# Router products with the padded router weights stationary on four column groups

## The reference

```python
x = layernorm(x + attention(x))          # 16 query heads, 4 key/value heads, head size 32, rotary on half
x = layernorm(x + mlstm(x, ctx, ctx))    # 16 heads, gates from [q, k, v], a running sum and maximum over time
x = layernorm(x + ffn(x))

# ffn: 16 experts, top 2, plus one shared expert
logits = flat @ router_w.T                               # 4096 x 512 by 512 x 16
scores = softmax(logits)
_, topk_idx = top_k(logits + router_bias, 2)
topk_scores = take_along_axis(scores, topk_idx); topk_scores /= topk_scores.sum(-1)
for e in range(16):
    out += combine[:, e] * ((silu(flat @ Wu[e]) * (flat @ Wg[e])) @ Wd[e])
out += (silu(flat @ Su) * (flat @ Sg)) @ Sd              # shared expert, inner size 512
```

## Time and profile before

| | us |
|---|---|
| median of 3 runs (2013.22 to 2020.41) | 2019.02 |
| the profiled execution, whole | 2020.32 |
| its span, first to last instruction | 2018.8 |
| TensorE busy | 1835.8 (91%) |
| VectorE busy | 1143.9 (57%) |
| ScalarE busy | 644.5 (32%) |
| GpSimd busy | 691.1 (34%) |
| mean granted TensorE clock | 0.961 of full |

### The profile page before, as it was taken

How to read it: one execution, slowest core, us unless ns; L and a number is a source line. 1 busy time by engine, 2 the same in 40 slices (tenths; PEclk the granted TensorE clock), 3 DMA queues, 4 the chain that set the end, 5 groups by cost and what they waited for, 6 DMA issues and landing times.

```text
span 2018.8 us, 35358 instructions
## 1 busy us (share of the span) xinstructions
PE 1835.8 (91%) x10992; PEld 1176.2 (58%) x10993; DVE 1143.9 (57%) x2407; ACT 644.5 (32%) x1355; POOL 691.1 (34%) x752
## 2 busy tenths in 40 slices
PE   3879999999999999999999999998789999999990
PEld 1556675766657576675766657576455444454440
DVE  1467766767677677767767676676432222222225
ACT  0142433335233352433435243342312212221224
POOL 4034232342423324232342423322224444444440
PEclk7789999999999999999999999998899999999995
DMA  8154342444424344242444424333415576656549
GB/s 283 43 119 113 59 122 73 93 113 92 122 63 102 89 100 121 62 122 73 92 114 92 122 56 109 82 85 73 147 43 129 111 187 171 126 120 145 93 74 342
DMA packets 151421, 225.94 MB, mean 112 GB/s; under 512 B 31889, under 2 KB 106641, under 8 KB 148817
## 3 DMA queue, kind: packets, MB, share of 16 engines
q1 hardware_dynamic: 102048, 132.94, 25.0%
q0 software_dynamic: 38112, 91.86, 19.9%
q10 hardware_dynamic: 11216, 0.61, 0.4%
HBM read 94.44 MB, written 48.57 MB: 71 GB/s over the span
## 4 chain that ended last, share of the span: by engine, by line
PE 77%; DVE 11%; issue 4%; ACT 3%; DMA 2%; SPq 1%; POOL 1%; DVEq 0%; ACTq 0%; POOLq 0%
PE ps L1606 14%; PE ps L1159 11%; PE ps L1097 8%; PE ps L1625 7%; PE ps L1386 6%; PE ps L1361 5%; PE ps L1245 4%; PE ps L1281 3%; PE ps L1350 3%; DVE arden L898 3%; PE ps L1228 3%; DVE smax L880 3%; PE ps L1111 2%; PE ps L1207 2%; PE ps L1594 2%
## 5 line engine op out<-in xcount | busy, mean ns | idle before, releaser
L1606 PE MATMUL ps<-ug_w,rowsT 128*128 x632 | 289.5, 601 | 8.0 <-SPq L1455 4.6
L489 POOL DMA_INDIRECT routed_ids<-pair_w,pos_w x64 | 64.1, 1001 | 453.8 <-DVE pair_w L776 409.4
L1606 PEld LDWEIGHTS ps<-ug_w,rowsT 128*128 128x128 f32 x632 | 121.5, 193 | 162.0 <-issue 162.0
L1495 POOL DMA_INDIRECT sum_rows<-y_sb,pairs x79 | 125.8, 1592 | 247.4 <-DVE y_sb L1573 125.1
L880 DVE TENSOR_REDUCE smax<-ps 128x2 f32<-128x512 f32 x256 | 163.5, 679 | 26.4 <-PE ps L1281 26.4
L1097 PE MATMUL ps<-wqkv_sb,xT_sb 128*128 128x256 f32 (+1 forms) x512 | 172.2, 489 | 6.0 <-DMA wqkv_sb<-in_wqkv 6.0
L898 DVE RECIPROCAL arden<-ps 128x256 f32<-128x256 f32 x64 | 112.5, 1758 | 114.2 <-PE ps L1350 104.6
L1561 DVE SCALAR_TENSOR_TENSOR silu<-tanh,ps 128x256 f32<-128x256 f32 x79 | 33.3, 421 | 249.8 <-ACT tanh L1516 249.8
L990 DVE SCALAR_TENSOR_TENSOR weighted<-ps,decay 128x384 f32<-128x384 f32 x256 | 140.1, 553 | 60.6 <-PE ps L1228 51.4
L633 ACT ACTIVATE decay<-ps,g_col 128x256 f32<-128x256 f32 x256 | 121.6, 475 | 137.8 <-PE ps L1209 100.6
L1281 PE MATMUL ps<-k_stack,q_stack 96*128 96x256 f32 x512 | 113.3, 326 | 41.8 <-DMA q_stack<-qkT_lo 25.8
(11 more groups left out here) (253 smaller groups left out, 3636.7 us busy)
## 6 DMA issues: line engine op xcount, KB each, us to landing
q_stack<-qkT_hi SPq DMA_DIRECT2D x128, 128.0 KB, 3.9
mk_stack<-ctxT_hi SPq DMA_DIRECT2D x128, 128.0 KB
mq_stack<-qkT_hi SPq DMA_DIRECT2D x128, 128.0 KB, 2.4
ug_w<-in_expert_ug SPq DMA_DIRECT2D x16, 1024.0 KB, 5.3
xT_sb<-in_xT SPq DMA_DIRECT2D x16, 512.0 KB, 3.2
x_sb<-in_x POOLq DMA_DIRECT2D x16, 512.0 KB, 3.8
ctxT_sb<-in_ctxT POOLq DMA_DIRECT2D x16, 512.0 KB, 3.9
ctx_sb<-in_ctx_in POOLq DMA_DIRECT2D x16, 512.0 KB, 7.7
```

Source lines behind the costliest of these rows:

```text
L1495: pool.indirect_dma_start(out=sum_dram, out_offset=bass.IndirectOffsetOnAxis(ap=tables.pairs[:, m, 0:1], axis=0), in_=y_sb[:, m % W, :], i ...
L1606: ins = nc.tensor.matmul(ps[:, 2 + k % 2, :], rowsT[:, k % 2, c, :], ug_w[:, bass.ds(slot, 1), c, :].rearrange("p o n -> p (o n)"), start= ...
```

## The change

The router weights become the stationary operand. `rw_sb` grows to 32 columns for each chunk, of which 16 are zeros. `route_chunks` makes four products of 256 tokens, one for each chunk of 128 rows, each on its own group of 32 columns of the array and so in its own 32 partitions of PSUM bank 4. These four partial products aren't accumulated. A new copy on ScalarE brings them into `lgT_sb`, which is the buffer `arden`. Then `route` makes two products, one for each token tile: `lgT_sb` is stationary, and `chunk_sum`, a matrix of zeros and ones made once at the start, sums the four chunks and turns the result to one row per token. `route_chunks` stands where `route` stood, and `route` now stands behind `gate_mm`.

```diff
-        rw_sb = sb("rw_sb", [P, KC, E])
+        rw_sb = sb("rw_sb", [P, KC, HD])
+        chunk_sum = sb("chunk_sum", [P, E])
...
+        lgT_sb = arden
...
-            late = [(wo_sb[:, :, :], wo), (rw_sb[:, :, :], router_w), (rb_sb[:, :], router_b.partition_broadcast(P)),
+            late = [(wo_sb[:, :, :], wo), (rw_sb[:, :, 0:E], router_w), (rb_sb[:, :], router_b.partition_broadcast(P)),
...
-            sp.wait_ge(consts.sem, 1)
+            sp.wait_ge(consts.sem, 2)
...
+            nc.gpsimd.memset(rw_sb[:, :, :], 0.0).then_inc(consts.sem, 1)
...
+                if w is not None:
+                    wait(act, lgT_ready, w, 1)
+                    nc.scalar.copy(lgT_sb[:, :], ps[:, 4, 0:S]).then_inc(lgT_done.sem, 1)
                 if y is not None:
                     wait(act, gabs_done, y, 1)
...
+            nc.vector.tensor_reduce(chunk_sum[:, :], id_sb[:, :].rearrange("p (j n) -> p n j", n=HD)[:, 0:E, :], AX.X, ALU.add)\
+                .then_inc(gwlo.sem, 1)
...
-                        lg = ps[:, 4, 0:ST * E].rearrange("p (t e) -> p t e", e=E)
+                        lg = ps[:, 4, S:S + ST * E].rearrange("p (t e) -> p t e", e=E)
...
+                def route_chunks():
+                    wait(pe, x2T_done, w, 1)
+                    for c in range(KC):
+                        ins = nc.tensor.matmul(ps[HD * c:HD * c + HD, 4, 0:S], rw_sb[:, c, :], x2T[:, c, :], start=True, stop=True)
+                    ins.then_inc(lgT_ready.sem, 1)
+
                 def route():
-                    wait(pe, x2T_done, w, 1)
+                    wait(pe, lgT_done, w, 1)
                     for t in range(ST):
-                        for c in range(KC):
-                            ins = nc.tensor.matmul(ps[:, 4, E * t:E * t + E], x2T[:, c, P * t:P * t + P], rw_sb[:, c, :],
-                                                   start=c == 0, stop=c == KC - 1)
+                        ins = nc.tensor.matmul(ps[:, 4, S + E * t:S + E * t + E], lgT_sb[:, P * t:P * t + P], chunk_sum[:, :],
+                                               start=True, stop=True)
                     ins.then_inc(lg_ready.sem, 1)
...
                 if w is not None:
-                    route()
+                    route_chunks()
                 if y is not None:
                     gate_mm()
+                if w is not None:
+                    route()
                 if w is not None:
                     ug(0)
```

More of the change, by code:

```diff
@@ L307, in attention_and_mlstm @@
         lg_ready, lg_done = sig("lg_ready", 1), sig("lg_done", 1)
+        lgT_ready, lgT_done = sig("lgT_ready", 1), sig("lgT_done", 1)
         top_step, choice_done = sig("top_step", 5 + TOPK), sig("choice_done", 1)
@@ L685, in _ @@
             nc.vector.tensor_scalar(filled[:, :], iota_sb[:, 0:E], float(N), None, ALU.mult).then_inc(gwlo.sem, 1)
-            dve.wait_ge(gwlo.sem, 7)
+            dve.wait_ge(gwlo.sem, 8)
             nc.vector.tensor_scalar(row_p[:, :], row_p[:, :], -1.0, float(P - 1), ALU.mult, ALU.add).then_inc(gwlo.sem, 1)
             nc.vector.tensor_scalar(lo_sign[:, :], is_lo[:, :], 2.0, -1.0, ALU.mult, ALU.add).then_inc(gwlo.sem, 1)
-            dve.wait_ge(gwlo.sem, 9)
+            dve.wait_ge(gwlo.sem, 10)
             for t in range(ST):
                 nc.vector.tensor_scalar(token_f[:, t:t + 1], row_p[:, :], float(P * t), None, ALU.add).then_inc(gwlo.sem, 1)
-            dve.wait_ge(gwlo.sem, 11)
+            dve.wait_ge(gwlo.sem, 12)
             dve.wait_ge(pro.sem, 2 + GQ)
@@ L1105, in gate_mm @@
                     if w is None:
-                        pe.wait_ge(gwlo.sem, 12)
+                        pe.wait_ge(gwlo.sem, 13)
                     n = 0
@@ L1184, in body @@
                         pe.wait_ge(first_in.sem, 11 * 16)
-                        pe.wait_ge(consts.sem, 3)
+                        pe.wait_ge(consts.sem, 4)
                     turn_qk()
```

## The result

The changed kernel takes 2051.83 us (median of 4 runs, 2050.01 to 2056.8) where the kernel before takes 2017.53 in the same comparison (4 runs, 2013.22 to 2020.41): 1.0175 of it, 95% interval 1.0157 to 1.0192. It is slower, as forecast (2056, range 2031 to 2077). The profiled execution took 2050.91, its span is 2049.3, and TensorE is busy 1827.7 us where it was 1835.8: less work on the engine that bounds the kernel, and a longer time.

The account below looks back on a forecast made before the run. TensorE bounds the kernel (77% of the chain), without slack over VectorE, ScalarE, VectorE at `ug(2)`. Terms: 30.8 + 5.4 + 0.4 - 0.8 + 1.0 = +36.8 on 2020.32 gives 2057.1, less 1.3 is 2055.8, said 2056; range 2031 to 2077.

Parts of the forecast that it names:

- TensorE's gain: Router products on TensorE: 1.69 us removed, 0.50 and 0.42 added, net gain 0.77 us a turn.
- The copy: ScalarE's new copy, 0.38 us, costs nothing under `gate_mm`; about 0.5 us would show without the gates in between.
- The later choice: On VectorE the logits' copy L921 comes behind the gates, at 967.81 instead of 966.19, later by 1.62 us.
- The hold: VectorE's cast L928 and L930 stand still until GpSimd's L475 ends at 971.22; L928 then ends at about 971.3.
- From exp to `ug(2)`: ScalarE's exp 2.8 us later, 0.62 absorbed, `hT` 2.2 later; TensorE idles 3.0 us; +2.2 a turn, 14 turns 30.8.
- The clock: TensorE's new idle time may drop the granted clock to 0.50, 1.8 us a time; three turns taken, 5.4 us.
- the wait without any fall: Rival: TensorE waits ahead of `ug(2)` but the granted clock never falls: 2050 us, chance 22%.
- The falls in most turns: Rival: the wait is there and the clock falls in most turns: 2068, up to 2076 us, chance 15%.
- The rest: Terms outside the full turns: turn without `b` +0.4, last turn -0.8, start +1.0 us.
- The turn without `b`: No L473 and L475 there; only the later choice counts, mostly covered by `ug(0)` and `ug(1)`: +0.4 us.
- The last turn: `route` at the low clock gets cheaper by 1.2 us, part of it given back: -0.8 us.
- The start: Router weights in 64-byte rows, 384 more DMA packets in a queue the first turn waits for: +1.0, between 0 and 1.9 us.

Follow-up runs that it names:

- The kernel with one column group: Changed kernel with its four chunk products accumulated on one group of 32 columns, only those 32 rows copied and multiplied: 2149.36 us, ratio 1.0271 to the kernel before.
- the last comparison: Third comparison, on a third chip (kernel before 2080.24 us): the changed kernel timed again unaltered, 2122.32 us, ratio 1.0213.
- the products-alone kernel: Changed kernel with `route` straight behind `route_chunks`, ahead of the gates: 2016.54 us, ratio 0.9996 to the kernel before.
- the first comparison: Comparison of the result, on the first chip: changed kernel 2051.83 us, ratio 1.0175 to the kernel before.
- the gates first: Kernel before with VectorE's L941 and L943 ahead of the choice and L944 behind it: 2094.43 us, ratio 1.0009.
- the position alone: Kernel before with its 16 old router products, only `route` moved behind `gate_mm`: 2040.76 us, ratio 1.0109.

## Why the prediction was right, point by point

**TensorE's gain.** Forecast 0.77 a turn. By the chain it is 1.69 - 0.57 - 0.36 = 0.76 for `route` itself. But from the end of the QKV products (985.28, before 964.03) to the start of `ug(0)` it is 3.69 us where it was 4.35, so 0.66. Timeline of TensorE, before and then after:

```profile
963.87 1.85 PE L1127 MATMUL ps<-rw_sb,x2T 128*128 128x16 f32 x16
...
968.38 1.89 PE L1159 MATMUL ps<-x2T,su_sb 128*128 128x256 f32 x8
```

```profile
985.21 0.64 PE L1135 MATMUL ps<-x2T,rw_sb 128*32 128x256 f32 x8
...
988.97 1.97 PE L1173 MATMUL ps<-x2T,su_sb 128*128 128x256 f32 x8
```

The missing 0.10 isn't in the gates, though their row in the chain says 2.92 for 2.82: from their first start to the next product's they take 2.83 (985.78 to 988.61) and took 2.81 (965.57 to 968.38). It lies ahead of the chunk products, of which the first starts 0.07 us ahead of the end of the QKV products, where L1127 started 0.16 ahead. The kernel with one column group has the same start, so it comes with a stationary operand of 32 columns and not with the four groups. The forecast had put the switch at 0.02. The difference had no effect, since TensorE waits anyway.

**The copy.** Hidden under the gates, as worked out; where they don't cover it, it costs 0.49, forecast "about 0.5".

**The later choice.** L930 ran at 989.16, 3.88 us behind the end of the QKV products at 985.28. The forecast had it at 967.81, 3.78 behind that end at 964.03. The 0.10 are the late start of the chunk products.

**The hold.** This was the step with the least support, a cast whose nearest row was L944. It was right to the size: 1.78 against an expected 1.8, and the order of events in the trace is the one forecast. The Trainium skill, "SBUF — State Buffer", section "Who interferes with whom", says that the pair of ports shared with GpSimd is given to one instruction for its whole length and that the other then stands still. The trace agrees: in four kernels the held cast ends within 0.03 us of GpSimd's subtraction, whether it was held for 0.28, 0.40, 1.61 or 2.0 us.

**From exp to `ug(2)`.** Idle time of 2.72, forecast 3.0; a turn of 88.78, forecast 88.9 (+2.13 against +2.2). 14 such turns make 29.8, where 30.8 was forecast.

**The clock.** This term failed. Three falls (5.4 us) were in the sum, and the profile of the result shows none at `ug(2)`. The second profile of the same kernel, in the last comparison, shows ten. The forecast said itself that the rows don't tell which of such idle times end in a fall, and three was right for neither profile. Of the two rivals priced for it, the wait without any fall (2050) is what the result shows, at 2051.83. The falls in most turns (2068, 1.024 of before) are what the last comparison shows, at 1.0213. The forecast lay so near the first because the term was small, and not because the clock was foreseen.

**The rest.** The turn without `b` cost 1.54 and not 0.4, but 1.27 of it are the one transfer shown with the result; without that it is near the forecast. The last turn gave -0.98 up to its `ug(0)`, forecast -0.8. In it, at the low clock, the timeline has the copy's wait in the open:

```profile
1492.43 1.04 PE L1141 MATMUL ps<-chunk_sum,arden 128*128 128x16 f32 x4 [0.49 <-ACT arden L579]
```

The start cost 2.2 and not 1.0. The page shows 384 more packets in the queue of the router weights (102432, 102048 before), but they are not where the time went: the first products of the attention behind the DMA wait start at 49.34 against 49.00, and by 84.89 against 84.95 that is gone. Of the 2.2, 1.4 are the low clock in one place, the chain's row

```profile
84.89 10.08 PE ps L1402 x16
```

where before has 8.65. Such a difference comes and goes between executions of one kernel; the products-alone kernel has 7.13 there. The next stretch is of the same kind. The granted clock is 0.50 from 114.7 to 131.8 in the changed kernel and from 111.9 to 122.2 before, and between 122 and 126 the distance of the two executions grows from 1.4 to 2.4. So at the first full turn the start had cost 2.4, and this turn itself lost only 1.9, with an idle time of 2.51. The forecast's 1.0, priced for the packets, has no run behind it.

**The sum.** 36.8 forecast: less 5.4 (falls), less 1.0 (turns), plus 1.2 (start), plus 1.1 (turn without `b`), less 0.2 (last turn), less 0.5 (behind it), less 1.5 (one irregular turn) is 30.5, as measured. The small terms, which are mostly clock and transfers that differ from one execution to the next, nearly cancelled each other. That is luck. What is left between 2056 and 2051.83 is mainly the falls.

## What to carry to other kernels

If a product's result is awaited by an engine with little slack, then fewer cycles on TensorE don't help when the product is moved behind other work to hide a copy. Ask first what is queued behind that wait on the consumer's engine. Then reorder this queue together with the product, or leave the product where it was. When the start of a step moves, look at what a neighbour that shares a port is doing in its new place; a step of 0.17 us cost 1.6 a turn only because it now met an instruction of 2.35 us. And measure a change whose new idle times are between 2 and 3 us on more than one chip.

## What the runs showed of the hardware that was not expected

- A very small step of VectorE is held as long as a large one. A cast of 128 x 4 elements waited up to 2.0 us (2.17 against 0.17) for GpSimd's subtraction, while the search for the maxima and that for their indices ran at 0.18 and 0.17 beside it, and so did the copy of the logits out of PSUM at 0.19.
- The same kernel with the same idle time of TensorE (2.72 and 2.73 us) kept its clock in 14 turns of 14 in the first comparison and lost it in 10 of 14 in the last, on the chip where the kernel before takes 2080.24 us; most falls cost 1.7 us. In the kernel with one column group, on the second chip, it was 2 of 14 behind 2.44 us. What decides it stays open.
- The kernel before is 3.7% slower on the second chip. Here is its chain of waits with the gates first, on that chip; in the first profile of the kernel before, the last two rows take 0.74 and 1.91:

```profile
874.04 2.10 another core or an unknown queue
...
877.40 1.22 PE ps L1331 x4
878.62 3.62 PE ps L1351 x32
```

The table of stretches for TensorE (stretch, length, busy, granted clock, DMA share, GB/s):

```profile
877.00:878.00 1.00, 0.60 (x3) 0.50 0.63 51
```

ScalarE stands idle for 2.1 us ahead of L616, which writes `mrden`, for something that the trace doesn't name (12 turns, 24.2 us). TensorE then idles for 2.56, and its clock is at 0.50 behind that. All idle times of this kind together are 42.2, 42.2, 42.2 and 41.9 us in the four profiles from the second chip, and 28.2 and 29.0 in the two from the third, with and without the change alike, which is why ratios and not times were compared. Of the first comparison's two profiles and the four from the first chip only that of the position alone has any (5.3 us). What ScalarE waits for was not found.
